# Column sweeps with the column innermost: rows become columns by an exchange in place, and columns run from a line buffer

## What is computed

```python
def step(carry, row):                       # one line from the line before it
    new = row + jax.nn.relu(conv1d(carry, w))   # 9 taps along the line, 64 x 64 channels
    return (new, new)
rows = jnp.transpose(x, (2, 0, 1, 3))       # 36 lines of 100
rows = sweep_fwd(rows, wd)                  # 35 steps
rows = sweep_bwd(rows, wu)                  # 34 steps; line 0 stays as it is
x = jnp.transpose(rows, (1, 2, 0, 3))
cols = jnp.transpose(x, (3, 0, 1, 2))       # 100 lines of 36
cols = sweep_fwd(cols, wr)                  # 99 steps
cols = sweep_bwd(cols, wl)                  # 98 steps
return jnp.transpose(cols, (1, 2, 3, 0))
```

## Time and profile before

| | us |
|---|---|
| median of 3 runs | 5338.52 (5335.29 to 5339.69) |
| the profiled execution, its own time | 5324.14 |
| the profiled execution, its span from the first to the last instruction | 5322.3 |
| PE busy | 4547.6 (85% of the span) |
| DVE busy | 1559.6 (29%) |
| ACT busy | 1453.8 (27%) |

### The profile page before, as it was taken

How to read it: one execution, slowest core, us unless ns; L and a number is a source line. 1 busy time by engine, 2 the same in 40 slices (tenths; PEclk the granted TensorE clock), 3 DMA queues, 4 the chain that set the end, 5 groups by cost and what they waited for, 6 DMA issues and landing times.

```text
span 5322.3 us, 93662 instructions
## 1 busy us (share of the span) xinstructions
PE 4547.6 (85%) x34633; PEld 3539.8 (67%) x34633; DVE 1559.6 (29%) x3214; ACT 1453.8 (27%) x5003; POOL 32.2 (1%) x73
## 2 busy tenths in 40 slices
PE   8899689986767998995999798888888888888887
PEld 2599689962324538995999335666666666666666
DVE  5755622223333476554222461000000000000000
ACT  3200310045554230004000882333333333333332
POOL 1000000000000000000000000000000000000000
PEclk8899899997778898997999995555555555555555
DMA  3100000011113350000000440000000000000000
GB/s 81 40 0 0 0 0 0 0 47 46 45 44 77 93 130 0 0 0 0 0 0 0 110 108 12 15 15 15 8 14 15 15 15 15 15 15 15 15 15 11
DMA packets 154784, 138.96 MB, mean 26 GB/s; under 512 B 87614, under 2 KB 154206, under 8 KB 154718
## 3 DMA queue, kind: packets, MB, share of 16 engines
q1 hardware_dynamic: 154718, 138.24, 10.9%
HBM read 79.18 MB, written 58.98 MB: 26 GB/s over the span
## 4 chain that ended last, share of the span: by engine, by line
PE 77%; ACT 12%; issue 6%; DVE 4%; ACTq 1%; SPq 0%; DMA 0%; DVEq 0%; POOL 0%; PEldq 0%; POOLq 0%
PE ps L704 18%; PE ps L549 17%; PE ps L625 15%; PE ps L526 15%; ACT xl L847 4%; ACT sums L749 4%; PE ps L488 2%; PE ps L510 2%; PE ps L500 2%; ACT img L719 2%; PE ps L569 1%; DVE img L895 1%; ACT xl L764 1%; PE ps L592 1%; PE ps L608 1%
## 5 line engine op out<-in xcount | busy, mean ns | idle before, releaser
L704 PE MATMUL ps<-xl,vt 65*32 65x16 f32 x14400 | 1066.9, 225 | 345.1 <-ACT xl L847 345.1
L704 PEld LDWEIGHTS ps<-xl,vt 65*32 65x32 f32 x14400 | 682.1, 141 | 617.2 <-ACT xl L847 415.4
L847 ACT ACTIVATE xl<-ps 64x16 f32<-64x16 f32 x3600 | 637.8, 177 | 1449.4 <-PE ps L704 1449.4
L549 PE MATMUL ps<-img,taps 128*128 x7880 | 920.2, 279 | 119.5 <-DVEq L735 70.6
L549 PEld LDWEIGHTS ps<-img,taps 128*128 128x128 f32 x7880 | 919.3, 190 | 120.7 <-issue 120.7
L625 PE MATMUL ps<-img,xl 128*64 x4808 | 988.3, 293 | 4.5 <-DVE vt L1092 4.1
L526 PE MATMUL ps<-split 128*128 128x400 f32 x4140 | 791.0, 353 | 13.5 <-DVE split L1023 13.5
L526 PEld LDWEIGHTS ps<-split 128*128 128x128 f32 x4140 | 783.9, 190 | 21.0 <-issue 14.6
L625 PEld LDWEIGHTS ps<-img,xl 128*64 128x64 f32 x4808 | 695.9, 206 | 96.0 <-issue 5.6
L1100 DVE TENSOR_TENSOR xl<-xl 64x480 f32<-64x480 f32 x120 | 115.6, 963 | 1972.9 <-PEq L701 1478.6
L749 ACT ACTIVATE sums<-img 64x200 f32 (+1 forms) x576 | 329.2, 572 | 466.6 <-DVE img L1007 458.3
(11 more groups left out here) (125 smaller groups left out, 1890.7 us busy)
## 6 DMA issues: line engine op xcount, KB each, us to landing
ring<-in_x_dram SPq DMA_DIRECT2D x288, 100.0 KB, 2.4
x_dram<-sums SPq DMA_DIRECT2D x288, 100.0 KB, 2.2
t_dram<-sums SPq DMA_DIRECT2D x144, 100.0 KB, 2.2
ring<-t_dram SPq DMA_DIRECT2D x144, 100.0 KB, 2.4
ring<-x_dram SPq DMA_DIRECT2D x144, 100.0 KB, 2.4
xl<-x_dram SPq DMA_DIRECT2D x30, 480.0 KB, 6.3
out_dram<-xl SPq DMA_DIRECT2D x30, 480.0 KB, 4.6
img<-in_L_ffn_weight_dram SPq DMA_DIRECT2D x4, 512.0 KB
```

Of the source, the lines that this page charges most:

```text
L549: last = pe.matmul(acc[:, :, lo:hi], taps[:, (k * NO + d + 2) * 128:(k * NO + d + 3) * 128], v[:, s0:s0 + HB, ds(at, 1), lo + d:hi + d].re ...
L704: last = pe.matmul(PS[s % 2][c * 32:(c + 1) * 32, t * B:(t + 1) * B], vt[:, c * 32:(c + 1) * 32], prev, start=False, stop=True, skip_group ...
L847: act.activation(yb[0:64, s, :, t], PS[s % 2][0:64, t * B:(t + 1) * B], ACT.Sigmoid).then_inc(step_y, 1)
```

## The change

The column layout is another one: `cols_view` now has the column `x` innermost, so that a column of an image is 18 elements with a step of 100, and a pair of rows (2m, 2m+1) of the row layout takes the same 100 elements per image as the same pair in the column layout. Rows become columns where they lie: the odd row of the low partitions and the even row of the high partitions change places, by way of `swap` in `xl`. ACT does this for pair after pair, from m = 17 down, as the backward row sweep finishes them; for the last pair one copy goes ahead of the last rows. `relayout` and DVE's part in it are gone. The column sweeps work on a line buffer `column[h]` in `xl`: PE reads its operand there, DVE writes the new column there (its second input is the column of `img`), and ACT copies it back into `img` (`act_columns`). DVE therefore also waits for `put_back`, and PE, DVE and ACT pass an `own` per step and half. `natural` reads elements that lie next to each other and writes with a step of 2. The image slots are the same for rows and columns (`FIRST_SLOT`).

```diff
         def cols_view(p, h):
-            return img[p[0]:p[1], h * HALF:(h + 1) * HALF].rearrange("p (b r j) -> p b r j", r=W, j=HP)
+            return img[p[0]:p[1], h * HALF:(h + 1) * HALF].rearrange("p (b j x) -> p b j x", j=HP, x=W)
...
         def pe_columns(pe, l, k):
-            view, s0, src, _, pairs = shape_of(k)
             with pe.Fori(0, STEPS[k]) as s:
-                at = pe.snap(src(s))
                 for h in range(2):
...
                     pe.wait_ge(state[l][h], s + LINES0[k])
+                    own(pe)
                     for n, d in enumerate(OFFS):
...
                         last = pe.matmul(acc[:, :, lo:hi], taps[:, (k * NO + d + 2) * 128:(k * NO + d + 3) * 128],
-                                         v[:, s0:s0 + HB, ds(at, 1), lo + d:hi + d].rearrange("p b r j -> p b (r j)"),
-                                         start=(n == 0), stop=(n == NO - 1))
+                                         column[h][:, :, lo + d:hi + d], start=(n == 0), stop=(n == NO - 1))
...
         def act_relayout(act, l):
-            relayout(act, l, 1, lambda o, a: act.activation(o, a, ACT.Copy))
-
-        def relayout(eng, l, h, move):
-            eng.wait_ge(state[l][h], LINES0[2] - 1)
-            eng.wait_ge(lo[l][h], LINES0[2] - 1)
-            eng.sem_inc(relaid[l][h], 1)
-            with eng.Fori(0, HB) as b:
-                eng.wait_ge(relaid[l][h], b + 1)
-                own(eng)
-                for hp in range(2):
-                    for wp in range(2):
-                        dst = cols_view(SIDE[hp], h)[:, ds(b, 1), wp::2, :].rearrange("p b w j -> p (b w) j")
-                        src = rows_view(SIDE[wp], h)[:, ds(b + 1, 1), hp::2, :].rearrange("p b r j -> p j (b r)")
-                        last = move(dst, src)
-                last.then_inc(relaid[l][h], 1)
-            eng.wait_ge(relaid[l][h], HB + 1)
-            eng.sem_inc(state[l][h], 1)
+
+            SWAPS = 3
+
+            def pair_part(h, side, m, row):
+                rows = img[SIDE[side][0]:SIDE[side][1], h * HALF:(h + 1) * HALF].rearrange("p (b m x) -> p b m x", m=HP, x=W)
+                s0 = FIRST_SLOT[l]
+                return rows[:, s0:s0 + HB, ds(m, 1), row * WP:(row + 1) * WP].rearrange("p b m x -> p b (m x)")
+
+            def exchange(h, m, moves, done):
+                for n, (to, frm) in enumerate(moves):
+                    if n or not isinstance(done, int):
+                        act.wait_ge(relaid[l][h], done + n)
+                        own(act)
+                    act.activation(to, frm, ACT.Copy).then_inc(relaid[l][h], 1)
+
+            def rows_done(h, count):
+                act.wait_ge(state[l][h], count)
+                act.wait_ge(lo[l][h], count)
+                own(act)
+
+            def swap_pair(m, count, done):
+                m = m if isinstance(m, int) else act.snap(m)
+                for h in range(2):
+                    odd, even = pair_part(h, 0, m, 1), pair_part(h, 1, m, 0)
+                    rows_done(h, count)
+                    exchange(h, m, ((swap[h], odd), (odd, even), (even, swap[h])), done)
+
+            swap_pair(HP - 1, LINES0[1] + 1, 0)
+            with act.Fori(0, HP - 2) as q:
+                swap_pair(q * -1 + (HP - 2), q * 2 + (LINES0[1] + 3), q * SWAPS + SWAPS)
+            done = (HP - 1) * SWAPS
+            for h in range(2):
+                act.wait_ge(relaid[l][h], done)
+                act.activation(swap[h], pair_part(h, 1, 0, 0), ACT.Copy).then_inc(relaid[l][h], 1)
+            for h in range(2):
+                odd, even = pair_part(h, 0, 0, 1), pair_part(h, 1, 0, 0)
+                rows_done(h, LINES0[2] - 1)
+                act.wait_ge(relaid[l][h], done + 1)
+                act.activation(even, odd, ACT.Copy).then_inc(relaid[l][h], 1)
+                act.wait_ge(relaid[l][h], done + 2)
+                act.activation(odd, swap[h], ACT.Copy).then_inc(relaid[l][h], 1)
+
+        def act_columns(act, l, k):
+            def step(s, x):
+                for h in range(2):
+                    act.wait_ge(state[l][h], s + (LINES0[k] + 1))
+                    own(act)
+                    act.activation(column_at(l, h, x), column[h], ACT.Copy).then_inc(put_back[l][h], 1)
...
+        def act_layer(act, l):
+            act_relayout(act, l)
+            act_columns(act, l, 2)
+            act_columns(act, l, 3)
+            for h in range(2):
+                act.wait_ge(put_back[l][h], 1 + STEPS[2] + STEPS[3])
...
                     for hp in range(2):
-                        dst = half(sums, h)[:, r * CH:(r + 1) * CH].rearrange("p (r w) -> p r w", w=W)[:, hp::2, :]
-                        src = cols_view(SIDE[hp], h)[:, ds(batch(i, u), 1), :, k * (CH_ROWS // 2):(k + 1) * (CH_ROWS // 2)]
-                        last = act.activation(dst, src.rearrange("p b w j -> p j (b w)"), ACT.Copy)
+                        rows = half(sums, h)[:, r * CH:(r + 1) * CH].rearrange("p (r j v) -> p r v j", j=WP, v=2)
+                        src = cols_view(SIDE[hp], h)[:, ds(slot, 1), k * (CH_ROWS // 2):(k + 1) * (CH_ROWS // 2), :]
+                        last = act.activation(rows[:, hp::2, :, :], src.rearrange("p b j (v x) -> p (b j) v x", v=2), ACT.Copy)
...
         def dve_columns(dve, l, k):
-            view, s0, _, target, pairs = shape_of(k)
-            with dve.Fori(0, STEPS[k]) as s:
-                at = dve.snap(target(s))
+            def step(s, x):
                 for h in range(2):
...
                     dve.wait_ge(conv[l][h], s + (STEPS0[k] + 1))
-                    dve.scalar_tensor_tensor(out=line, in0=acc, scalar=0.0, in1=line, op0=ALU.max, op1=ALU.add
+                    dve.wait_ge(put_back[l][h], s + (STEPS0[k] - STEPS0[2] + 1))
+                    own(dve)
+                    dve.scalar_tensor_tensor(out=column[h], in0=acc, scalar=0.0, in1=column_at(l, h, x), op0=ALU.max, op1=ALU.add
                                              ).then_inc(state[l][h], 1)
...
             dve_rows(dve, l, 1)
-            relayout(dve, l, 0, lambda o, a: dve.tensor_copy(o, a))
+            for h in range(2):
+                dve.wait_ge(relaid[l][h], 3 * HP)
+                dve.tensor_copy(column[h], column_at(l, h, 0)).then_inc(state[l][h], 1)
+                dve.sem_inc(put_back[l][h], 1)
```

58 lines of the change are left out of this document (36 added, 22 removed).

## The result

| | us |
|---|---|
| the kernel before, median of 4 runs | 5336.91 (5330.32 to 5339.69) |
| the changed kernel, median of 4 runs | 5120.58 (5116.51 to 5123.98) |
| ratio | 0.9605, 95% interval 0.9583 to 0.9627 |
| the changed kernel's profiled execution (its span) | 5116.51 (5114.7) |

The change saves 216.3 us between the medians and 207.6 between the two profiled executions. The direction was right, but 5120.58 lies 11 us under the low end of the range (5132) and 43 under the forecast (5164). Four mechanisms were forecast; all four gains are there, but one of them was sized by a bound that did not hold.

What follows compares the result with a forecast made beforehand. PE alone was taken to pace the sweeps, with a 62 us hole between them in each layer. 5338.5 - 116.6 (relayout) + 1 (column ends) - 36 (norm 1) - 23 (norm 3) gave 5164 us; range 5132 to 5226.

Steps and rivals of the forecast that it cites:

- Step 4, norm 1: Norm 1 behind the columns: chunks go from 3.43 us to SP's 2.86, ACT's 2.47 not binding; 36 us saved.
- Step 4, `natural`'s write: ACT's copies in `natural`: contiguous reads, writes with an 8-byte step nearly free by L847; 0.38 us against 0.58 each.
- rival (a): Norms behind the columns gain nothing, as ACT's writes with a step cost what such reads do; 5223 us, chance 0.11.
- Step 4, norm 3: Norm 3 behind the columns: 71 intervals fall from 236.3 us to norm 2's pace of 3.00 each; 23 us saved.
- Step 1: Relayout between row and column sweeps goes: PE's hole shrinks to 2.8 us, saving 58.3 us per layer, 116.6 in all.
- Step 2: ACT's exchange copies, 57 us per layer, hide behind the backward row sweep; cost 0.
- rival (d): The exchange does not hide behind the row sweep; all of it exposed gives 5278 us; chance 0.04.
- Step 3: Column step: added DVE and ACT work fits some 0.5 us of room, cost 0; column ends add 1 us in all.
- rival (c): Column hand-over between conv and state exceeds its room, 39 us per 0.1 us over; likely 5200 us, chance 0.06.
- low bound of 5137: Whole kernel: the forecast's fast end, with 60 us a layer from the relayout, 48 from norm 1, 33 from norm 3.
- bound of 5195: Whole kernel: the slow end of the forecast's own bounds, in us; the forecast within its bounds had chance 0.75.

## Why the prediction was wrong

The account between the profiled executions: 174.6 forecast, 207.6 measured. The missing 33.0 are 13.2 in norm 1, 6.0 in norm 3, 7.4 in norm 0, 5.9 from the last row to the last column and 0.5 in the rest.

- **Step 4, norm 1, is the step that failed**, by its term of 36 us, the largest part of the 33.0. The sentence was "But ACT's 2.47 is then not the bound", with SP's 2.86 us a chunk in its place. I had worked out ACT's chunk rightly: it runs at 2.50. But a queue that lags for two chunks at a group's start is not shown to be the bound of the whole group. SP needs 2.73 in the steady part and has the bumps, where ACT's chunk takes 3.1 to 4.3 us, to catch up; the run with three DMAs, whose groups are the same, shows it, and so do the groups of 44.7 to 44.9 us with all four DMAs, 2.64 a chunk. What holds the group is ACT's chunk, as the run with the 72-byte step shows (57.8 again), and with it waits for PE that come with the clock. And I took the gain of group one (9 of 9.7) for all four, though group two took 60.1. Measured were 45.2 in the groups and 3.5 in the rest of the stage, where the routing's clock decides.
- **Step 4, `natural`'s write**: 0.38 us was right (380 ns), its reason was not. L847 does not write with a step of 120 bytes: `yb` is laid out `(s t b)`, so its 16 elements lie next to each other. The row says nothing on writes with a step, and rival (a) had no row against it; only the rule that the prediction cites from the Trainium skill spoke for the price. That it came out is no merit of the row.
- **Step 4, norm 3**: the pace of norm 2 was the nearest row, for the reason given (PE's work of the same kind), and PE is the fullest engine now. Its size was off: 71 intervals at 3.00 were forecast (213), and 2.92 was measured (207.3, against 236.3). I had no reason for the last 0.08 us, and have none now.
- **Step 1** was right in each detail: the hole is 2.4 us against 2.8. What it left out is the clock behind the hole. Before, PE came back at half speed; the window of the kernel before behind its hole has 0.88 on the mean:

```profile
682.00:700.00 18.00, 18.00 (x138) 18.00 (x139) 4.01 (x13) 0.00 (x0) 0.00 (x0) 0.88 0.00 0
```

  Now it does not fall in layer 0, and in layer 1 for some 3.4 us (by the 0.57 of the 4 us from 2302 on). In the other three profiles of the change it falls behind both holes, behind both and behind neither, and a sweep is 1.4 us longer where it does. By the lengths of the column sweeps (457.5 and 457.6 before, plus the half-step of 1.16 that lay in the hole; 455.5 and 457.0 now) this gives 3 and 2 us. I had read the 0.51 of the earlier trace rows and costed only its idle time.
- **Step 2**, cost 0, was right; rival (d) fell with it, and its price of 57 us a layer was 68 in the run.
- **Step 3**, cost 0, was right in its result and wrong in two of its reasons. DVE's read with a step costs 0.10 us, which L1026 did not show: that is a copy of one source, this an operation of two, and whether that makes the difference is not shown. The room left was not 0.5 us but, by the estimate above, under 0.1 where a restart of PE costs little. Had the change put another 0.3 us on DVE, 57 us a layer would have been lost, rival (c) in full. The end of the columns is near the forecast's 0.5: 0.91 us from DVE's last instruction to ACT's table load, 0.26 before.
- The Trainium skill's rule (SBUF — State Buffer, section Specifications), that a 16-byte line wants two hits and each cross to a new line pays, held in three places that were open: steps of 8 bytes are free (380 ns), ACT's write and DVE's two-source read with a step of 400 bytes pay (465 against 323, 410 against 308). It did not hold for DVE's one-source read (L1026), nor for ACT's read to and fro between two runs, which crosses at each element and takes 378 ns. I had set it aside for DVE by the one row, and should have kept it as the bound.
- **Rival (a)** is out by the 380 ns, and (c) by columns of the same length as before.
- **The median.** I carried 14.4 us from the profiled execution to the median; after the change that distance is 4.1, so about 10 us of the miss are this step. It had no reason: in the later comparisons the profiled execution lay 6.4 us above the median (the kernel before) and 24.4 above it (the change).
- **The range.** Against its low bound of 5137, which already held 60 us a layer, 48 and 33, the measured time is 17 us lower, and there norm 1 plays hardly a part: 10.3 are the carried distance, 7.4 norm 0, which stood at nothing, 2.5 the relayout, 0.7 norm 1 and 0.5 the rest, less 4.5 of norm 3. So the bounds of the mechanisms held but for a few us, and what the range lacked was a term for the scatter of the clock. The bound of 5195 has no working: its own terms (55 us a layer, +10, nothing in the norms) add up to some 5240.

## What to carry to other kernels

A queue that lags in one part of a loop is a bound only if it lags on the mean. Compare its demand with the whole loop's, bumps included, before letting it cap a gain. When a hole of an engine goes, price the clock behind it as well as its length, and where stages that the change does not touch scatter by several us from one profile to the next, give the range a term for it. Before taking a row as kin, read the layout of its tile in the code. And before spending "room" on a critical hand-over, subtract what the change itself adds: of the 0.5 us here less than 0.1 was left by the estimate.
